# Two transformer blocks on one core: a row scatter spread more densely over the attention heads, and one routing batch's ranks taken three heads earlier

## The chip, the cores and the metric

The kernel runs on one core of one Trainium2 chip. The metric is the device time of one execution in microseconds (us). Five engines work beside each other, each in the order of its own queue: TensorE (PE, with its weight loads shown as PEld), VectorE (DVE), ScalarE (ACT), GpSimd (POOL) and SyncE (SP). They meet only at semaphores.

## The reference, cut to what matters

The input is x with 8 sequences of 256 tokens and 256 features. Block 0 is full attention of 16 heads and a gated low rank layer. Block 1 is causal attention of 16 heads in 4 groups and a mixture of 32 experts, of which each token takes 4, with one more expert that all tokens share:

```python
x = x + attention0(layernorm(x)); x = x + lora_ffn(layernorm(x))
x = x + attention1(layernorm(x))                 # causal, 8 sequences, 16 heads
h = layernorm(x)                                 # 2048 rows of 256
scores = sqrt(softplus(h @ router_w.T))
idx = top_k(scores + expert_bias, 4)
topv = scores[idx] / (scores[idx].sum() + 1e-20)
x = x + sum_k topv[k] * expert[idx[k]](h) + shared_expert(h)
```

The change concerns the way in which rows of h come to their experts.

## The kernel before

**Routing in five batches.** While block 1's attention runs over its 8 sequences (b = 0 to 7, 16 heads each, s = 0 to 15), the sequences that are already through it are routed. `BATCHES` groups them: sequences 0-1, 2-3, 4-5, 6 and 7 are batches 0 to 4 (the change's "second" and "third" batch are batches 1 and 2 by this count). Each batch goes through these steps, at heads given by tables `{(b, s): batch}`: router logits (`LOGITS_AT`, PE), softplus and root (ACT, DVE), the four best experts (`TOP_AT`, DVE), `pick_four` (`PICK_AT`, DVE: L2001 one-hot, L2004 sum, which releases `chosen_ready`), `ranks` on PE and `find_slots` on DVE (both by `RANKS_AT`). `ranks` (L1494 to L1501) counts with matmuls how many rows chose each expert before; `find_slots` (L2020 to L2028) turns that into the row numbers `slot` and releases `slots_ready`.

**The scatter.** For each of a batch's token tiles (128 rows) and each of the four choices, POOL issues one indirect DMA (`scatter`, L890) of 128 rows of 1,040 bytes to DRAM, `rows_by_expert`. That is 16 for each of batches 0 to 2 and 8 for each of batches 3 and 4: 64 in all. `SCATTERS` holds, for batches 0 to 2, (first head by number b*16+s, steps, of, count): scatter n goes behind the exponential of head `first + n * steps // of`. What is left of batch 2 and all of batches 3 and 4 goes behind the loop. SP waits for all 64 to land (`scattered`) before it loads the first block of rows for the experts (L732).

**What else is in POOL's queue.** At head 8 of each sequence stands `scale_rows(b - 1)` (L880, L881), the inverse deviation of the sequence before. ACT's `normalize_row` (L1043) waits for it at heads 9 and 10 of the last sequences, PE's `turn_rows` for that, and so on to the logits. Behind the loop the same step for sequence 7 stands between two of batch 2's scatters.

**The rest around the heads.** Each head is `scores` on PE (L1423, L1426), an exponential on ACT (L1095), and for every four heads `values` on PE (L1447, L1450). Score tiles, router logits, ranks and turned sums share a ring of three PSUM banks, in the order of use that `ring_uses` lists: who takes a bank waits until its use before the last two is read. At head 5 PE turns the sums of the sequence before (`turn_back`, L1461), and DVE divides them and takes row statistics (`divide`, L2035 to L2050, L1957 to L1963). The shared expert's first quarter also lies in the last sequences: its tanh at (7, 1), DVE's `shared_hidden` (L1864, L1868) at (7, 7), PE's `shared_down` (L1540) at (7, 9) and (7, 11).

**Behind the loop** PE does, in this order, `values`, `turn_back(7)`, the shared expert's `shared_up(1)` and `(2)` (L1529), `turn_rows(7)`, logits of batch 4, ranks of batch 3, `shared_down(1)`, `shared_up(3)`, ranks of batch 4, `count` (L1509), `shared_down(2)`. DVE's `find_slots` of batch 4 is followed by the block tables (`count_blocks`, `place_blocks`, L1882 to L1929), which every engine's expert loop needs. In the loop over blocks, rows are read from `rows_by_expert`, multiplied (L1613 to L1635) and scattered again by POOL (L926).

Of the kernel before, what the change touches and what calls it, by code (L numbers as in the profile page):

```python
# [162 lines left out]
SCORES_AT = {(3, 6): 0, (5, 6): 1, (6, 14): 2}  # L163
ROOT_AT = {(3, 8): 0, (5, 8): 1, (6, 15): 2}
TOP_AT = {(3, 10): 0, (5, 10): 1, (7, 0): 2}
PICK_AT = {(3, 13): 0, (5, 13): 1, (7, 2): 2}
RANKS_AT = {(4, 1): 0, (6, 1): 1, (7, 6): 2}
UP_AT, CLIP_AT, TANH_AT, HIDDEN_AT, DOWN_AT, ADD_AT = ((6, 7), (6, 9)), (6, 10), (7, 1), (7, 7), ((7, 9), (7, 11)), (7, 12)
SCATTERS = ((66, 7, 4, 16), (98, 11, 8, 16), (121, 11, 8, 5))


def norms_at(b):
# [3 lines left out]
def rows_at(b):  # L176
    return {SEQS - 2: 11, SEQS - 1: 12}.get(b, 14)


def scatters_at(i):  # L180

    return [(j, n) for j, (first, steps, of, count) in enumerate(SCATTERS) for n in range(count) if first + n * steps // of == i]

# [6 lines left out]
def ring_uses(layer):  # L190
    uses = [("m", 0, 0)]
    for b in range(SEQS):
        for h in range(HEADS):
# [3 lines left out]
            if b + 1 < SEQS and h == TURN_MAX:  # L197
                uses.append(("m", b + 1, 0))
            if layer and (b, h) in RANKS_AT:
                uses.append(("k", RANKS_AT[b, h], 0))  # L200
            if layer and b and h == rows_at(b):
# [23 lines left out]
def two_block_kernel(nc, x_in, wqkv0, wproj, bproj, wffn, debias, wdown, center, slope,  # L225
                     wqkv1, bq1, bk1, bv1, router, ebias, wexp_in, out):
    ctx = ExitStack()
    with ctx:
# [99 lines left out]
        work = cut(exps, 0, TILES * TOPK * EXPERTS, "p (t k e) -> p t k e", t=TILES, k=TOPK)  # L328
        SMALL = ONE_AT + (EXPERTS - 2) * EW
        most = max(size for _, size in BATCHES) * QT * EXPERTS  # L330
        lg, soft, ex, ln = (cut(arena, SMALL + i * most, most, tile_expert, t=most // EXPERTS) for i in range(4))
        sbi = cut(arena, SMALL + 2 * most, most, tile_expert, t=most // EXPERTS)
# [431 lines left out]
        def _(pool):  # L764
# [111 lines left out]
            def scale_rows(b):  # L876

                at = slice(b * QT, (b + 1) * QT)
                pool.wait_ge(rows_var, b + 1)
                then(pool.tensor_tensor(rstd[:, at], var[:, at], mhalf[:, 0:QT], ALU.pow))  # L880
                pool.tensor_tensor(shift[:, at], nmean[:, at], rstd[:, at], ALU.mult).then_inc(rows_scaled, 1)  # L881

            def scatter(j, start, end, after=None):

                pool.wait_ge(slots_ready, j + 1)
                for n in range(start, end):
                    t, k = divmod(BATCHES[j][0] * QT * TOPK + n, TOPK)
                    if after is not None:
                        pool.wait_ge(exp_ready[1], after + 1)
                    pool.indirect_dma_start(xs, bass.IndirectOffsetOnAxis(ap=slot[:, t, k:k + 1], axis=0),  # L890
                                            xn4[:, t, :], None).then_inc(scattered, 16)
# [13 lines left out]
            for b in range(POOL_MASKS, SEQS):  # L905
                for h in range(HEADS):
                    if h == ROWS_VAR:
                        scale_rows(b - 1)
                    for j, n in scatters_at(b * HEADS + h):
                        scatter(j, n, n + 1, b * HEADS + h)  # L910
            scatter(2, SCATTERS[2][3], 7)
            pool.wait_ge(divided[1], SEQS * QT)
            scatter(2, 7, 9)
            scale_rows(7)
            scatter(2, 9, 16)
            scatter(3, 0, 8)
            scatter(4, 0, 8)

# [298 lines left out]
        def _(pe):  # L1217
# [188 lines left out]
            def turn_maxima(n, b):  # L1406
                wait_ring(n, ("m", b, 0))
                pe.wait_ge(neg_ready[n], b + 1)
                dst = st_bank[RING_AT[n]["m", b, 0] % 3]
                for qt in range(QT):  # L1410
                    ins = pe.transpose(dst[0:2 * HEADS, qt * P // 2:(qt + 1) * P // 2].bitcast(BF16),
                                       neg[:, qt, :, :].rearrange("p a h -> p (a h)"), identb[:, :])
                ins.then_inc(negT_ready[n], 1)
# [73 lines left out]
            def ranks(j):  # L1487

                first, size = BATCHES[j]
                t0, n = first * QT, size * QT  # L1490
                wait_ring(1, ("k", j, 0))
                pe.wait_ge(chosen_ready, j + 1)
                dst = st_bank[RING_AT[1]["k", j, 0] % 3]
                pe.matmul(dst[:, 0:n * EXPERTS], before[:, :], chosen[:, t0:t0 + n, :].rearrange("p t e -> p (t e)"),  # L1494
                          start=True, stop=False, skip_group_check=True)
                for t in range(t0):
                    pe.matmul(dst[:, 0:n * EXPERTS], onesb[:, :],
                              chosen[:, t, :].unsqueeze(1).broadcast_to([P, n, EXPERTS]),
                              start=False, stop=False, skip_group_check=True)
                for t in range(1, n):  # L1500
                    ins = pe.matmul(dst[:, t * EXPERTS:n * EXPERTS], onesb[:, :],  # L1501
                                    chosen[:, t0:t0 + n - t, :].rearrange("p t e -> p (t e)"),
                                    start=False, stop=(t == n - 1), skip_group_check=True)
                ins.then_inc(ranks_ready, 1)
# [40 lines left out]
            def attention(n):  # L1545
# [7 lines left out]
                for b in range(SEQS):  # L1553
# [6 lines left out]
                    for s in range(HEADS):  # L1560
# [8 lines left out]
                        if s == TURN_MAX and b + 1 < SEQS:  # L1569
                            turn_maxima(n, b + 1)  # L1570
                        if n and (b, s) in RANKS_AT:
                            ranks(RANKS_AT[b, s])
                        if n and b and s == rows_at(b):
# [115 lines left out]
        def _(dve):  # L1689
# [289 lines left out]
            def top_four(j):  # L1979
                first, size = BATCHES[j]  # L1980
                t0, n = first * QT, size * QT
                dve.wait_ge(root_ready, j + 1)
                step(1, dve.tensor_tensor(sbi[:, 0:n, :], sco[:, t0:t0 + n, :],
                                          ebb[:, :].unsqueeze(1).broadcast_to([P, n, EXPERTS]), ALU.add))
                for t in range(n):
                    ins = dve.max(m8[:, t0 + t, :], sbi[:, t, :])
                step(1, ins)
                for t in range(n):
                    ins = dve.max_index(i8[:, t0 + t, :], m8[:, t0 + t, :], sbi[:, t, :])
                step(1, ins)  # L1990
                step(1, dve.tensor_copy(pk8[:, 0:n, 0:TOPK], i8[:, t0:t0 + n, 0:TOPK]))
                for t in range(n):
                    ins = dve.max(m8[:, t0 + t, :], pk8[:, t, :])
                step(1, ins)
# [58 lines left out]
            def attention(n):  # L2053
                for b, k in first_pairs(n):
                    pair(n, b, k)
                for b in range(SEQS):
                    for s in range(HEADS):
# [12 lines left out]
                        if n and (b, s) in TOP_AT:  # L2070
                            top_four(TOP_AT[b, s])
                        if n and (b, s) in PICK_AT:
                            pick_four(PICK_AT[b, s])
                        if n and (b, s) in RANKS_AT:
                            find_slots(RANKS_AT[b, s])
                        if n and (b, s) == ADD_AT:
# [201 lines left out]
```

## Time and profile before

| what | value |
|---|---|
| median of 3 runs | 653.28 us (646.13, 653.28, 654.76) |
| the profiled execution's own time | 649.37 us |
| its span, first to last instruction | 647.6 us |
| mean granted TensorE clock | 0.951 |
| POOL busy, instructions | 243.1 us (38%), 341 |
| PE busy | 557.5 us (86%) |

Block 1's attention with its routing ends at about 428 us of the span, the first expert block begins at 471 us, and the rest is the expert loop and the final sums. All times of rows below count from the span's start. A timeline row gives start, length, what the instruction is, how many of it were merged, and in brackets how long the engine had been idle and what released it. PE's starts are recorded and its ends modelled, so a semaphore that a matmul sets can be seen by others later than the row suggests.

### The profile page before, as it was taken

To read this page: it belongs to the slowest core of one execution; us is meant where nothing else is said; L and a number is where in the kernel's file an instruction comes from. 1 tells how busy PE (TensorE), PEld (TensorE's weight loads), DVE (VectorE), ACT (ScalarE), POOL (GpSimd) and SP (SyncE) were. 2 spreads that over 40 slices of the span, in tenths; PEclk is the share of its full clock that TensorE was granted. 3 is DMA by queue.
4 is the path that set the end of the run, shared out by engine and by line. 5 is a ranking of instruction groups with operands and counts; after the bars stand their busy time and mean duration, and the time that the engine had idled before them with its cause. 6 is when DMAs were issued, how large, how long until landed. Compare 5 with 4: busy or idle time off the path is not lost.

```text
span 647.6 us, 14149 instructions
## 1 busy us (share of the span) xinstructions
PE 557.5 (86%) x4202; PEld 397.7 (61%) x4203; DVE 431.6 (67%) x1296; ACT 352.7 (54%) x902; POOL 243.1 (38%) x341
## 2 busy tenths in 40 slices
PE   4999898799879789898988987884689999889986
PEld 2565465466458764576756755552567787777864
DVE  4558787688236886676787773452757777767855
ACT  2452476577736578356665546442146665556662
POOL 2353010000603213275545534476525555445530
PEclk9999699899999889999999987798789999989999
DMA  7499879400000006777214151163335454434499
GB/s 249 162 302 284 232 197 271 128 4 2 3 1 1 2 0 179 226 208 229 117 63 171 69 212 68 57 222 148 115 108 149 147 151 144 143 118 147 147 362 343
DMA packets 49536, 95.21 MB, mean 147 GB/s; under 512 B 8580, under 2 KB 40524, under 8 KB 46924
## 3 DMA queue, kind: packets, MB, share of 16 engines
q1 hardware_dynamic: 41804, 75.34, 37.7%
q0 software_dynamic: 7680, 19.21, 7.9%
q8 instruction: 29, 0.48, 0.3%
q14 instruction: 23, 0.19, 0.1%
HBM read 58.54 MB, written 35.59 MB: 145 GB/s over the span
## 4 chain that ended last, share of the span: by engine, by line
PE 45%; DVE 20%; issue 11%; POOL 8%; DMA 7%; ACT 6%; another core or an unknown queue 1%; DVEq 0%; ACTq 0%; POOLq 0%; SPq 0%
PE banks L1423 6%; PE banks L1379 5%; PE banks L1240 4%; POOL rows_by_expert L890 4%; PE banks L1444 4%; DVE mx L1943 3%; PE banks L1315 3%; PE banks L1624 3%; DVE mx L1940 3%; POOL results_by_rank L926 3%; DMA arena<-negT 3%; DVE attn_w L2137 2%; PE banks L1246 2%; DMA arena<-results_by_rank 2%; PE banks L1635 2%
## 5 line engine op out<-in xcount | busy, mean ns | idle before, releaser
L1095 ACT ACTIVATE arena<-banks 128x512 f32<-128x512 f32 (+1 forms) x256 | 130.1, 549 | 88.7 <-PE banks L1423 50.4
L926 POOL DMA_INDIRECT results_by_rank<-attn_w,goes x80 | 78.1, 976 | 82.8 <-issue 49.7
L1423 PE MATMUL banks<-arena 98*128 98x256 bf16 (+1 forms) x512 | 90.5, 271 | 18.1 <-DMA arena<-negT 5.5
L1940 DVE TENSOR_REDUCE mx<-banks 128x4 f32<-128x1024 f32 x64 | 76.1, 1221 | 21.7 <-PE banks L1379 21.6
L1379 PE MATMUL banks<-arena 96*128 96x256 bf16 (+1 forms) x512 | 83.0, 267 | 5.4 <-DVE mx L1940 2.5
L890 POOL DMA_INDIRECT rows_by_expert<-arena,bpb x64 | 63.5, 992 | 59.1 <-ACT arena L1095 26.4
L1624 PE MATMUL banks<-arena,attn_w 128*128 x320 | 84.7, 388 | 0.3 <-issue 0.3
L1423 PEld LDWEIGHTS banks<-arena 98*128 98x128 bf16 x512 | 44.4, 102 | 52.0 <-ACT arena L1095 16.7
L1943 DVE TENSOR_REDUCE mx<-banks 128x4 f32<-128x1024 f32 (+1 forms) x48 | 57.5, 1221 | 20.3 <-PE banks L1383 19.4
L1379 PEld LDWEIGHTS banks<-arena 96*128 96x128 bf16 x512 | 50.6, 100 | 21.6 <-issue 5.6
L1624 PEld LDWEIGHTS banks<-arena,attn_w 128*128 128x128 f32 x320 | 55.9, 195 | 5.3 <-issue 0.9
L1635 PE MATMUL banks<-arena,attn_w 128*128 x160 | 50.5, 397 | 7.2 <-ACT attn_w L1179 3.8
L2137 DVE TENSOR_SCALAR attn_w<-banks 128x256 f32<-128x256 f32 x80 | 34.0, 425 | 29.6 <-issue 14.1
L1167 ACT ACTIVATE attn_w<-attn_w 128x128 f32<-128x128 f32 x80 | 24.8, 310 | 51.6 <-DVE attn_w L2137 41.7
L811 POOL DMA_DIRECT2D arena<-negT x24 | 12.2, 511 | 105.9 <-ACT negT L1027 105.8
L1635 PEld LDWEIGHTS banks<-arena,attn_w 128*128 128x128 f32 x160 | 28.5, 191 | 19.4 <-issue 16.3
L1383 PE MATMUL banks<-mask_s,identb 128*128 128x128 bf16 x256 | 40.1, 220 | 0.0
L1444 PE MATMUL banks<-arena 128*17 128x256 f32 x512 | 35.6, 397 | 1.1 <-ACT pvs L1036 1.1
L1613 PE MATMUL banks<-ident,pvs 128*128 128x128 f32 x160 | 31.6, 280 | 4.1 <-DMA pvs<-rows_by_expert 4.0
L898 POOL TENSOR_SCALAR_AFFINE_SELECT arena<-arena 128x256 f32<-128x256 f32 x64 | 26.2, 420 | 22.8 <-ACT arena L1095 22.7
L803 POOL TENSOR_TENSOR arena<-arena 128x512 bf16<-128x512 f32 x16 | 18.3, 1160 | 41.7 <-ACT arena L938 41.7
L1173 ACT ACTIVATE attn_w<-banks 128x256 f32<-128x256 f32 x80 | 31.0, 387 | 3.1 <-DMA results_by_rank<-attn_w,goes 2.8
(246 smaller groups left out, 1107.8 us busy)
## 6 DMA issues: line engine op xcount, KB each, us to landing
arena<-parts_dram SPq DMA_DIRECT2D x72, 256.0 KB, 4.0
pvs<-rows_by_expert SPq DMA_DIRECT2D x80, 130.0 KB
parts_dram<-arena SPq DMA_DIRECT2D x24, 384.0 KB, 3.0
arena<-results_by_rank SPq DMA_DIRECT2D x6, 1024.0 KB, 10.4
arena<-in SPq DMA_DIRECT2D x2, 2304.0 KB
rows_by_expert<-zero SPq DMA_DIRECT2D x1, 4160.0 KB, 23.4
arena<-in SPq DMA_DIRECT2D x2, 1920.0 KB
arena<-in SPq DMA_DIRECT2D x3, 768.0 KB
```

Source lines behind the costliest of these rows:

```text
L890: pool.indirect_dma_start(xs, bass.IndirectOffsetOnAxis(ap=slot[:, t, k:k + 1], axis=0), xn4[:, t, :], None).then_inc(scattered, 16)
L926: pool.indirect_dma_start(ys, bass.IndirectOffsetOnAxis(ap=goes[:, j:j + 1], axis=0), yb[j], None).then_inc(y_stored[j], 16)
L1095: act.activation(p_ring[n][:, i % P_RING, :], st_bank[RING_AT[n]["s", b, s] % 3][:, 0:P_WIDTH[n]], ACT.Exp, scale=HD ** -0.5).then_inc(exp ...
L1379: ins = pe.matmul(dst[:, a * nk:(a + 1) * nk], q_rows(n, slice(0, STACK), h0 + a, b, qt * P, P), k_rows(n, slice(0, STACK), h0 + a, b, 0, ...
L1383: ins = pe.matmul(dst[:, a * nk + nk - P:(a + 1) * nk], identb[:, :], mask_s[:, :], start=False, stop=True)
L1423: ins = pe.matmul(dst[:, at:at + SEQ - q0], keys, q_rows(n, slice(0, ROWS), s, b, q0, SEQ - q0), start=True, stop=(n == 0 or b < POOL_MASKS))
L1444: ins = pe.matmul(pv_bank[rows, col:col + SEQ], vals, p[:, kt * SEQ:(kt + 1) * SEQ], start=(kt == 0), stop=(kt == QT - 1))
L1624: ins = pe.matmul(bank[2 + p][:, 0:2 * INNER], xbT[:, p, k, :], experts[:, bass.ds(e * EW + k * 2 * INNER, 2 * INNER)], start=(k == 0), st ...
L1635: pe.matmul(bank[6 + p][:, 0:D], hidT[:, p, :], experts[:, bass.ds(e * EW + 2 * KD * INNER, D)], start=True, stop=True).then_inc(y_ready, 1)
L1940: ins = dve.tensor_reduce(out, src.rearrange("p (q h k) -> p q h k", q=QT, k=nk), AX.X, ALU.max)
L1943: ins = dve.tensor_reduce(out, src.rearrange("p (h k) -> p h k", k=nk), AX.X, ALU.max)
L2137: dve.tensor_scalar(gu[:, p, :, :].rearrange("p g i -> p (g i)"), bank[2 + p][:, 0:2 * INNER], CLAMP, -CLAMP, ALU.min, ALU.max).then_inc(g ...
```

## The change

Batch 1's scatters come one for 9/8 heads in place of 11/8, still from head 98. Batch 2's come one for each head from head 117 in place of 11/8 from head 121; so 11 of its 16 stand in the loop in place of 5, and the numbers of the pieces behind the loop follow (2, then 2, `scale_rows(7)`, 1; before 2, then 2, `scale_rows(7)`, 7). Batch 2's `pick_four` moves from (7, 2) to (7, 1), and its `ranks` and `find_slots` from (7, 6) to (7, 3). The ring of PSUM banks follows the tables.

```diff
@@ -163,10 +163,10 @@
 SCORES_AT = {(3, 6): 0, (5, 6): 1, (6, 14): 2}
 ROOT_AT = {(3, 8): 0, (5, 8): 1, (6, 15): 2}
 TOP_AT = {(3, 10): 0, (5, 10): 1, (7, 0): 2}
-PICK_AT = {(3, 13): 0, (5, 13): 1, (7, 2): 2}
-RANKS_AT = {(4, 1): 0, (6, 1): 1, (7, 6): 2}
+PICK_AT = {(3, 13): 0, (5, 13): 1, (7, 1): 2}
+RANKS_AT = {(4, 1): 0, (6, 1): 1, (7, 3): 2}
 UP_AT, CLIP_AT, TANH_AT, HIDDEN_AT, DOWN_AT, ADD_AT = ((6, 7), (6, 9)), (6, 10), (7, 1), (7, 7), ((7, 9), (7, 11)), (7, 12)
-SCATTERS = ((66, 7, 4, 16), (98, 11, 8, 16), (121, 11, 8, 5))
+SCATTERS = ((66, 7, 4, 16), (98, 9, 8, 16), (117, 1, 1, 11))
 
 
 def norms_at(b):
@@ -908,11 +908,11 @@
                         scale_rows(b - 1)
                     for j, n in scatters_at(b * HEADS + h):
                         scatter(j, n, n + 1, b * HEADS + h)
-            scatter(2, SCATTERS[2][3], 7)
+            scatter(2, SCATTERS[2][3], 13)
             pool.wait_ge(divided[1], SEQS * QT)
-            scatter(2, 7, 9)
+            scatter(2, 13, 15)
             scale_rows(7)
-            scatter(2, 9, 16)
+            scatter(2, 15, 16)
             scatter(3, 0, 8)
             scatter(4, 0, 8)
```

POOL's queue from batch 1's scatters on (L890 are scatters, L880 and L881 are the two instructions of a `scale_rows`):

```order
-L890 DMA rows_by_expert<-arena,bpb 65536x260 x8
-L880 TENSOR_TENSOR rstd<-var,mhalf 128x2
-L881 TENSOR_TENSOR shift<-nmean,rstd 128x2
-L890 DMA rows_by_expert<-arena,bpb 65536x260 x11
-L880 TENSOR_TENSOR rstd<-var,mhalf 128x2
-L881 TENSOR_TENSOR shift<-nmean,rstd 128x2
 L890 DMA rows_by_expert<-arena,bpb 65536x260 x9
 L880 TENSOR_TENSOR rstd<-var,mhalf 128x2
 L881 TENSOR_TENSOR shift<-nmean,rstd 128x2
-L890 DMA rows_by_expert<-arena,bpb 65536x260 x23
+L890 DMA rows_by_expert<-arena,bpb 65536x260 x13
```

The piece goes on with `scale_rows` and runs of 12 and 17. So the runs of scatters ahead of `scale_rows(5)`, `(6)`, `(7)` and behind it were 8, 11, 9 and 23 long and are now 9, 13, 12 and 17: six scatters less stand behind `scale_rows(7)`.

DVE's queue in the last sequence, from batch 2's `pick_four` (L2001 to L2008) on; L2020 to L2028 is its `find_slots`, L2035 to L2044 is `divide`:

```order
 L2004 TENSOR_REDUCE products<-arena 128x128
 L2008 SCALAR_TENSOR_TENSOR arena<-ffn_w,tok 128x4x4
+L2020 SCALAR_TENSOR_TENSOR arena<-iota,banks 128x128
+L2025 TENSOR_TENSOR arena<-arena 128x512
+L2027 TENSOR_REDUCE pk<-arena 128x16
+L2028 CAST bpb<-pk 128x16
 L2035 RECIPROCAL rec<-banks 128x16
 L2044 TENSOR_TENSOR arena<-banks,rec 128x256
```

`find_slots` now stands ahead of the divisions and row statistics of sequence 6, where it stood behind them. `pick_four` keeps its place in the queue: nothing stood between (7, 1) and (7, 2).

PE's queue in the last sequence, around the place where the ranks of batch 2 (L1494 to L1501) now stand; each four rows of L1423 and L1426 are one head's scores, L1461 is `turn_back`:

```order
 L1501 MATMUL banks<-products,onesb 128x64
 L1501 MATMUL banks<-products,onesb 128x32
+L1423 MATMUL banks<-arena 128x256
+L1426 MATMUL banks<-mask_t,identb 128x128
+L1423 MATMUL banks<-arena 128x128
+L1426 MATMUL banks<-mask_t,identb 128x128
+L1423 MATMUL banks<-arena 128x256
+L1426 MATMUL banks<-mask_t,identb 128x128
+L1423 MATMUL banks<-arena 128x128
+L1426 MATMUL banks<-mask_t,identb 128x128
+L1461 MATMUL banks<-ident,pvs 128x128 x8
+L1423 MATMUL banks<-arena 128x256
```

The added rows, the scores of heads 4 and 5, `turn_back(6)` and the scores of head 6, stood ahead of the ranks and now stand behind them.

## Rows read from the trace of the kernel before

**Rows 1.** Cores view: span and mean granted TensorE clock.

```profile
core 0: 647.6 us, clock 0.951
```

**Rows 2.** Chain of work ending last, 395 to 430 us: start, length, what.

```profile
408.39 0.22 PE banks L1494
...
410.36 0.30 DVE arena L2020
...
412.94 0.70 DVE attn_w L1868
413.68 2.07 PE banks L1540 x4
```

**Rows 3.** The same chain, 436 to 472 us.

```profile
451.05 3.68 issue
...
464.31 4.06 DMA rows_by_expert<-arena,bpb
...
469.13 2.16 DMA pvs<-rows_by_expert
```

**Rows 4.** Timeline, POOL: start, length, engine, line, operation, tiles [idle before <-releaser].

```profile
409.37 0.72 POOL L880 TENSOR_TENSOR rstd<-var,mhalf 128x2 f32<-128x2 f32 x1
...
412.74 1.08 POOL L890 DMA_INDIRECT rows_by_expert<-arena,bpb  x1 [2.37 <-DVE bpb L2028]
...
425.06 0.99 POOL L890 DMA_INDIRECT rows_by_expert<-arena,bpb  x1 [0.30 <-issue]
428.05 1.29 POOL L890 DMA_INDIRECT rows_by_expert<-arena,bpb  x1 [2.00 <-DVE arena L2044]
...
430.62 0.73 POOL L880 TENSOR_TENSOR rstd<-var,mhalf 128x2 f32<-128x2 f32 x1
...
441.20 0.96 POOL L890 DMA_INDIRECT rows_by_expert<-arena,bpb  x1 [0.30 <-issue]
...
450.08 0.96 POOL L890 DMA_INDIRECT rows_by_expert<-arena,bpb  x1 [0.30 <-issue]
454.95 1.15 POOL L890 DMA_INDIRECT rows_by_expert<-arena,bpb  x1 [3.90 <-DVE bpb L2028]
```

**Rows 5.** Source view of the scatter line.

```profile
L890 POOL DMA_INDIRECT rows_by_expert<-arena,bpb x64: 957/963/1428, 343.4 to 464.3; - x64
```

**Rows 6.** Timeline, ACT.

```profile
403.28 0.87 ACT L1095 ACTIVATE arena<-banks 128x384 f32<-128x384 f32 x2
```

**Rows 7.** Timeline, DVE.

```profile
402.26 1.02 DVE L2004 TENSOR_REDUCE products<-arena 128x128 bf16<-128x512 f32 x1
...
405.63 0.26 DVE L2035 RECIPROCAL rec<-banks 128x16 f32<-128x16 f32 x1 [2.27 <-PE banks L1461]
...
409.11 0.18 DVE L1963 TENSOR_SCALAR nmean<-mv 128x2 f32<-128x2 f32 x1
...
437.95 0.38 DVE L2028 CAST bpb<-pk 128x8 uint32<-128x8 f32 x1
...
442.13 0.68 DVE L1860 TENSOR_SCALAR attn_w<-banks 128x512 f32<-128x512 f32 x1
453.33 0.22 DVE L2020 SCALAR_TENSOR_TENSOR arena<-iota,banks 128x64 f32<-128x64 f32 x1 [10.53 <-remote]
...
466.50 0.14 DVE L1922 TENSOR_SCALAR trips_i<-trips_i 1x1 int32<-1x1 int32 x1
```

**Rows 8.** Timeline, PE.

```profile
403.82 0.39 PE L1423 MATMUL banks<-arena 98*128 98x256 bf16 x1 [2.63 <-ACT arena L1095]
...
409.26 0.37 PE L1501 MATMUL banks<-products,onesb 128*128 128x96 bf16 x3
...
413.68 2.07 PE L1540 MATMUL banks<-arena,attn_w 128*128 128x256 f32 x4 [2.52 <-DVE attn_w L1868]
...
445.11 0.18 PE L1501 MATMUL banks<-products,onesb 128*128 128x32 bf16 x1
...
446.20 0.21 PE L1509 MATMUL banks<-products,onesb 128*128 128x32 bf16 x2 [0.55 <-issue]
```

## The prediction, made before the changed kernel ran

> **What bounds the kernel now.** I read the page first: one core, 647.6 us of span, PE busy for 86% of it at a mean granted clock of 0.951 [rows 1]. PE's share is an average over stages, so I went on to the chain of waits in the two stretches that the change touches. In the last sequence of block 1's attention [rows 2] the chain goes from batch 2's ranks on PE (408.39) to `find_slots` on DVE (410.36), on to the shared expert's hidden product (412.94, ended 413.64), and back to PE's `shared_down` at 413.68: there PE stands behind a DVE queue. Behind the attention [rows 3] the chain is POOL's scatters, one by one, then 3.68 us of POOL idle at 451.05, the last eight scatters, 4.06 us from the last one's start to its landing, and 2.16 us of the first block's load. Everything of the expert loop stands behind that. Then the timelines of POOL, DVE, ACT and PE one at a time, to see who has slack.
>
> What is to be seen in POOL's [rows 4]: the last scatter ahead of the final division runs at 425.06, two follow the division from 428.05 on, `scale_rows(7)` runs at 430.62, and from there 15 scatters run without a gap: seven of batch 2, then batch 3's eight from 441.20 to 451.04. That is a full queue: batch 3's row numbers were made at 438.33 [rows 7] (the cast at 437.95) and waited 2.9 us for POOL. Batch 4's eight begin at 454.95, for they had to wait for their row numbers.
>
> **The change, part by part.**
>
> *Batch 2's ranks and slots at head 3.* The pick at (7, 1) in place of (7, 2) moves nothing: DVE has nothing between the two. Its sum ended at 403.28 [rows 7], so the ranks at head 3 can begin on PE at about 403.4. PE was idle there anyway: it waited 2.63 us, until 403.82, for the exponential that ACT could only begin at 403.28 [rows 6, 8]. The ranks take 1.24 us (408.39 to 409.63 [rows 2, 8], at the lower clock) and so end at 404.65. What is late next are the scores of heads 4 and 5 and `turn_back(6)`, which stand behind them: scores of head 5 from about 405.1 in place of 403.82, so up to 1.3 us late. In return PE is rid of the same 1.24 us at 408.39, and stands level again by head 7. `find_slots` starts 0.73 us behind the ranks' last row (409.63 to 410.36), so at 405.4. With the two hidden products of 0.70 each it took 410.36 to 413.64, so alone 1.9: it ends at 407.3. The divisions and statistics of sequence 6, which started at 405.63 and were through at 409.29 (3.66 us [rows 7]), now start at 407.3 and end at 411.0. The hidden products follow at once and end at 412.4 in place of 413.64: **1.2 us sooner**, and PE waits for exactly these. `scale_rows(6)` moves from 409.37 to about 411.9, since it also has a scatter ahead of it; ACT normalizes at heads 9 and 10, and PE turns those rows only at head 12, behind 2.07 us of `shared_down` [rows 2] and three heads, so I cost this at nothing. If that cover is gone it costs PE 1.3 to 2.6 us.
>
> *Denser scatters in the loop.* Scatters do not block PE, DVE or ACT, and a scatter ahead of `scale_rows` costs it at most one pace. Batch 1 is through about 4 us sooner (three heads' worth). Batch 2's row numbers come at 407.3, where its first scatter ran at 412.74 before [rows 4]. From there to the end of the attention, which now comes at about 426.8, are 19.4 us. The 13 scatters and `scale_rows(6)` that POOL has to do in them need 13 times the full queue's pace of 1.27 us (below) and 1 us, 17.5 in all, so POOL keeps up. No more instructions are issued: 64 scatters before and after, 957/963/1428 ns at least, in the middle and at most [rows 5].
> The Trainium skill (SBUF — State Buffer, section "SBUF: two separate sides") speaks against such a move: it says that POOL and DVE share a pair of SBUF ports, locked by one for a whole instruction, so that descriptors for POOL's own DMAs may wait for a DVE instruction in a two-port mode. By it, six scatters moved from a stretch in which DVE idles to one in which it works could each be as long as the longest row, 1.43 in place of 0.96, or 2.8 us of POOL. The row's middle of 963 ns, with most of the 64 beside DVE's work, speaks for nothing, and where they now stand POOL waits for exponentials anyway.
>
> *Six scatters less behind `scale_rows(7)`.* The pace in a full queue is (450.08 - 441.20) / 7 = 1.27 us, so six are 7.6 us of POOL. But one of the terms comes short: batch 3's row numbers. They hang on `scale_rows(7)`, which moves with the 1.2 us of the attention from 430.62 to 429.4, and so come at 437.1. POOL does the one scatter left and then idles until 437.15. Batch 3's scatters thus start at 437.15 in place of 441.20 and end at 447.0 in place of 451.04: **4.05 us sooner**, of which 1.2 are those above.
>
> *Batch 4's start* decides what of this reaches the end. Before, DVE's `find_slots(4)` began at 453.33 after 10.53 us of idle, though PE's rows of the ranks end at 445.29 and those of the count at 446.41 [rows 7, 8]. The releaser is not told. So PE's semaphore came 8 us behind its row, for a reason that the trace does not show. Bounds from both sides: a hold of fixed length moves by 1.2 only; no hold at all puts the row numbers at about 446, ahead of POOL, and batch 4's start moves from 454.95 to 447.3, by 7.65. Between them: the hold ended 2.3 us behind the last scatter of batch 3 (451.04), and if it goes with the scatters all moves by 4.05. If ordinary executions have no such hold, before had POOL at 451.35 and the changed kernel has it at 447.3, which is 4.05 again. I take **4.05**, which two of the four readings give.
>
> Behind it nothing else ends later: the block tables on DVE (453.33 to 466.64, 13.3 us [rows 7]) start from the same semaphore as batch 4's row numbers and are through 1.7 us before the last scatter lands (464.31 + 4.06 = 468.37 [rows 3]). That keeps its distance.
>
> **The sum.** 649.37 - 4.05 = 645.3 against the profiled execution's own time (span 647.6 and 1.8 around it). The median of the runs, 653.28, lies 3.9 above it, and their lowest, 646.13, 3.2 below. The four times of the kernel have a mean of 650.9, and I put the forecast there: 650.9 - 4.05 = 646.9, said as 647.
>
> **The rivals.**
>
> *The hold stays as long as it is* (25%). PE's count and ranks are the same, and so is what stands ahead of them. Then the tail gains only the 1.2 us: 649.7. For it speaks that batch 4's first scatter was released by DVE and not by POOL's own queue; against it that no hold of this size stands behind batch 3's ranks, with nearly as many matmuls.
>
> *The hold goes* (15%). It would belong to this one execution, or to PE's work beside a full POOL queue. Then 7.65 us: 643.2.
>
> *Slower: PE waits at head 3* (18%). The ranks at head 3 stand ahead of heads 4 and 5, which ACT would otherwise have begun at 403.82 and before. If the 1.3 us on `turn_back(6)`, and a further 1.3 us because `find_slots` stands ahead of the divisions and a scatter ahead of `scale_rows(6)`, are not caught up, then the attention ends 2.6 us later, and with a hold of fixed length so does everything: 653.5. It decides from the point where PE's head 9 scores (their bank waits for sequence 6's divisions two uses before) start later than 411.0, so that `shared_down` no longer waits for DVE. Against it: PE waited there 2.52 us for DVE before [rows 8].
>
> *The change does nothing to time* is the case of the first rival without its 1.2 us and is counted there.
>
> **How the numbers follow.** Forecast 42%, the others as above. The range should hold 8 in 10: its low end is 643.2 less 1.5 for the spread of a median, which I take as half of the 3.2 by which the lowest run lies under the profiled one; the high end is 653.5 and 1. So 641.7 to 654.5. 2% of the time is 13 us, about what a measurement of this kernel can tell from no change; even the best case lies within it. Only where it falls together with a set of low runs is the change faster by that much (5%), and slower by 2% needs 13 us that no case has (2%).
>
> **What would show it.** In the changed kernel's profile: PE's ranks rows (L1494) in the idle gap at about 403.4, `shared_down` waiting about 1.2 us for DVE instead of 2.5, `scale_rows(7)` at about 429.4, POOL idle for some 6 us between the one scatter behind it and batch 3's first at about 437, and batch 4's first close behind batch 3's last. Wrong would be: the first block later than 469.5 (then the hold or the wait at head 3), or `scale_rows(7)` at 431 or later (then the in-loop part failed and the gain from the tail is at most what POOL's queue gives).

## The result: slower by 0.9% where the forecast was faster by 0.6%

| | before | after |
|---|---|---|
| median (20 runs each, side by side) | 650.31 us | 654.44 us |
| span of the profiled execution | 647.6 us | 652.8 us |
| granted clock | 0.951 | 0.953 |

The ratio is 1.0092, with a 95% interval of 1.0067 to 1.0116. It compares fast runs alone, the slower state being left out, and is not the quotient of the two medians, which is 1.0064. The forecast of 647.0 was the mean of the kernel's four times then known, 650.9, less 4.05 us. The time lies at the upper edge of the range, but its direction is that of the rival with 18%, and the mechanism is neither the forecast's nor that rival's.

The cores of the kernel after, which answer to [rows 1]:

```profile
core 0: 652.8 us, clock 0.953
```

POOL's timeline of the kernel after, as [rows 4] (start, duration, line, idle time before it with what ended it):

```profile
414.93 0.73 POOL L880 TENSOR_TENSOR rstd<-var,mhalf 128x2 f32<-128x2 f32 x1
...
416.46 1.04 POOL L890 DMA_INDIRECT rows_by_expert<-arena,bpb  x1 [0.52 <-issue]
417.80 0.96 POOL L890 DMA_INDIRECT rows_by_expert<-arena,bpb  x1 [0.30 <-issue]
...
424.14 0.96 POOL L890 DMA_INDIRECT rows_by_expert<-arena,bpb  x1 [0.31 <-issue]
427.93 0.96 POOL L890 DMA_INDIRECT rows_by_expert<-arena,bpb  x1 [2.83 <-ACT arena L1095]
...
435.12 0.73 POOL L880 TENSOR_TENSOR rstd<-var,mhalf 128x2 f32<-128x2 f32 x1
...
436.28 1.04 POOL L890 DMA_INDIRECT rows_by_expert<-arena,bpb  x1 [0.16 <-issue]
444.12 0.96 POOL L890 DMA_INDIRECT rows_by_expert<-arena,bpb  x1 [6.80 <-DVE bpb L2028]
...
454.39 1.15 POOL L890 DMA_INDIRECT rows_by_expert<-arena,bpb  x1 [0.43 <-DVE bpb L2028]
...
463.46 0.96 POOL L890 DMA_INDIRECT rows_by_expert<-arena,bpb  x1 [0.30 <-issue]
```

Three things are to be seen. Seven scatters now follow each other without a gap while the attention still runs (416.46 to 425.10). `scale_rows(7)` comes at 435.12 and not at 429.4. And what was foretold for the tail is there in form: one scatter, 6.80 us of idle time, batch 3, and batch 4 right behind it. The last scatter even starts sooner than before (463.46 against 464.31). POOL's queue is thus not what made it late.

Rows of ACT, of DVE and of PE in the kernel after, from their timelines:

```profile
426.66 0.49 ACT L1095 ACTIVATE arena<-banks 128x384 f32<-128x384 f32 x1 [6.11 <-remote]
467.00 1.09 ACT L1060 ACTIVATE arena<-banks 128x512 f32<-128x512 f32 x2 [9.47 <-remote]
```
```profile
407.50 0.29 DVE L2020 SCALAR_TENSOR_TENSOR arena<-iota,banks 128x128 f32<-128x128 f32 x1 [3.36 <-remote]
426.60 0.22 DVE L1969 COPY arena<-banks 128x64 f32<-128x64 f32 x1 [8.25 <-remote]
...
464.07 0.19 DVE L1882 COPY wd<-banks 128x32 f32<-128x32 f32 x1 [7.21 <-remote]
...
473.10 0.15 DVE L1925 SCALAR_TENSOR_TENSOR stored_i<-wd,iota 1x12 int32<-1x12 f32 x1
```
```profile
404.20 0.27 PE L1494 MATMUL banks<-products,before 128*128 128x128 bf16 x1 [2.82 <-DVE products L2004]
...
414.13 1.13 PE L1540 MATMUL banks<-arena,attn_w 128*128 128x256 f32 x4 [0.60 <-DVE attn_w L1868]
...
469.31 2.02 PE L1517 MATMUL banks<-ident,vec 128*128 128x96 f32 x8 [7.12 <-DVE vec L1908]
...
478.41 0.63 PE L1613 MATMUL banks<-ident,pvs 128*128 128x128 f32 x4 [1.62 <-ACT arena L1060]
```

"Remote" marks a wait whose releaser is not told. By the program these are waits for a semaphore of PE's, and it came long after its matmul's row: the count's rows (L1509) end at 451.2, and DVE goes on at 464.07. As the ends of PE's rows are modelled, they do not tell whether the matmuls ended late or only their semaphores came late; "late semaphore" stands for both below. Before, there was one such wait of size, the 10.53 us of [rows 7]. Now ACT's exponential waits 6.11 us and DVE's copy 8.25 us beside the seven scatters, and in the tail DVE's count 7.21 us and ACT's turned sums 9.47 us beside the last sixteen. The attention's last statistics end at 434.41 instead of 429.91 (+4.5 us), the block tables at 473.4 (one row behind the last shown) instead of 466.9, the same instruction (+6.5), and the first block starts at 478.41 instead of 471.33 (+7.1). The way from the late count to the first block is in PE's rows: PE waits 7.12 us for a value of the tables (L1517, 469.31), `shared_down(3)` stands behind that in its queue, ACT takes its result (`L1060`), and PE's first block waits for ACT, no longer for the scattered rows. The expert blocks give 1.9 us back, and the span is 5.2 us longer.

### The profile page after: what moved, and what is told of

Its sections match the earlier page's. It is cut to its first block, busy times and chain, and to the rows that moved or that the text cites. A ratio compares the mean times of both kernels' runs of the same rounds, so it can differ in the third digit from the quotient of the medians.

```text
span 652.8 us, 14155 instructions
## 1 busy us (share of the span) xinstructions
PE 556.3 (85%) x4202; PEld 395.7 (61%) x4203; DVE 431.2 (66%) x1296; ACT 352.5 (54%) x902; POOL 243.2 (37%) x341
## 4 chain that ended last, share of the span: by engine, by line
PE 42%; DVE 23%; issue 10%; ACT 7%; DMA 7%; POOL 5%; another core or an unknown queue 4%; DVEq 0%; ACTq 0%; POOLq 0%; SPq 0%
PE banks L1423 5%; PE banks L1379 4%; PE banks L1240 4%; PE banks L1624 4%; DVE mx L1943 3%; PE banks L1444 3%; DMA arena<-negT 3%; DVE mx L1940 3%; PE banks L1315 3%; POOL results_by_rank L926 3%; PE banks L1246 2%; PE banks L1635 2%; DMA arena<-results_by_rank 2%; DVE attn_w L2137 2%
## 5 line engine op out<-in xcount | busy, mean ns | idle before, releaser
L1423 PE MATMUL banks<-arena 98*128 98x256 bf16 (+1 forms) x512 | 90.2, 270 | 18.9 <-DMA arena<-negT 7.3
L890 POOL DMA_INDIRECT rows_by_expert<-arena,bpb x64 | 63.6, 994 | 57.6 <-ACT arena L1095 27.3
L1624 PE MATMUL banks<-arena,attn_w 128*128 x320 | 82.6, 381 | 0.7 <-ACT attn_w L1162 0.4
L1423 PEld LDWEIGHTS banks<-arena 98*128 98x128 bf16 x512 | 43.8, 101 | 53.8 <-ACT arena L1095 13.9
L1624 PEld LDWEIGHTS banks<-arena,attn_w 128*128 128x128 f32 x320 | 54.5, 190 | 5.3 <-issue 1.2
L1635 PE MATMUL banks<-arena,attn_w 128*128 x160 | 50.0, 394 | 7.4 <-ACT attn_w L1179 3.8
L1635 PEld LDWEIGHTS banks<-arena,attn_w 128*128 128x128 f32 x160 | 28.2, 189 | 19.6 <-issue 16.5
```

What stands on the lines that cost most here:

```text
L1423: ins = pe.matmul(dst[:, at:at + SEQ - q0], keys, q_rows(n, slice(0, ROWS), s, b, q0, SEQ - q0), start=True, stop=(n == 0 or b < POOL_MASKS))
L1624: ins = pe.matmul(bank[2 + p][:, 0:2 * INNER], xbT[:, p, k, :], experts[:, bass.ds(e * EW + k * 2 * INNER, 2 * INNER)], start=(k == 0), st ...
L1635: pe.matmul(bank[6 + p][:, 0:D], hidT[:, p, :], experts[:, bass.ds(e * EW + 2 * KD * INNER, D)], start=True, stop=True).then_inc(y_ready, 1)
```

## The experiments

The kernels ran in sets, each set on one chip, with runs of the kernel before among them; a ratio is to those, with its 95% interval. A "650 us set" is one in which before takes about 650 us (its median was 649.9 and 652.3 in the two below, 650.3 in the result), a "634 us set" one in which it takes 632.8 to 634.8. That there are two kinds was not expected, and turned out to be the main finding. The experiments stand in the order in which they ran.

### First set (650 us): which part of the change costs

The part that moves the ranks alone (`e1`):

```diff
-PICK_AT = {(3, 13): 0, (5, 13): 1, (7, 2): 2}
-RANKS_AT = {(4, 1): 0, (6, 1): 1, (7, 6): 2}
+PICK_AT = {(3, 13): 0, (5, 13): 1, (7, 1): 2}
+RANKS_AT = {(4, 1): 0, (6, 1): 1, (7, 3): 2}
```

> The picks, ranks and slots of batch 2 as in the changed kernel, all scatters as before. Theory R (an unbroken run of POOL's scatters holds back the arrival of PE's semaphores): nothing runs back to back in the last eight heads, so no 6 us gap behind the logits; time as before or up to 1.2 us less (ratio 0.998 to 1.000). Theory P (the new place of ranks in PE's queue makes the stall): the gap of about 6 us on ACT behind head 14 of the last sequence is there, ratio about 1.008. Theory N (the stalls fall by chance and the two kernels differ by their tails): gap or not by chance, ratio within 0.5% of before.

Measured: 649.21 us, 0.9972 [0.9934, 1.0010]. The ranks' new place does not cost the 0.9%. In its trace the wait of before ahead of batch 4's slots is still there (10.6 us), and none over 1.1 us lies in the last two sequences. From the first statistics of block 1 to the last ones the attention takes 125.8 us, against 128.3 in before and 132.2 in the kernel after (one trace each).

The change with batch 1's scatters left as before (`e2`), and batch 1's alone (`e3`):

```diff
-SCATTERS = ((66, 7, 4, 16), (98, 9, 8, 16), (117, 1, 1, 11))    # after
+SCATTERS = ((66, 7, 4, 16), (98, 11, 8, 16), (117, 1, 1, 11))   # e2
-SCATTERS = ((66, 7, 4, 16), (98, 11, 8, 16), (121, 11, 8, 5))   # before
+SCATTERS = ((66, 7, 4, 16), (98, 9, 8, 16), (121, 11, 8, 5))    # e3
```

> The changed kernel with batch 1's scatters at 11/8 heads again, batch 2's still one for each head from head 117. Theory R: POOL's run in the last eight heads stays (it is even longer, since batch 1's last ones lie there too), so the gap of 5 to 6 us stays and the ratio is 1.008 or more. Theory P: the same as the changed kernel, 1.009. Theory N: within 0.5% of before. If batch 1's density were the cause, the ratio would be 1.000 or less.

> The kernel before with batch 1's scatters one for 9/8 heads and nothing else changed. Theory R: POOL is a little denser in sequence 6, runs of three to six scatters; a gap of 1 us at most, ratio 1.000 to 1.003. Theory P: ratio 1.000. If it carries the loss: 1.006 or more.

Measured: e2 1.0049 [1.0013, 1.0084], e3 1.0036 [1.0001, 1.0070]. Each seems to carry a part. But the controls below read 0.9956 and 0.9976 for the kernel before against itself, so neither is told from 1 for certain. What e2's trace shows is surer. It has the same run of seven scatters, ACT's exponentials wait 13.0 us there in three waits, and the tables are late as in the kernel after (472.3); e3, without the run, has one wait of 2.4 us of ACT's and one of 10.7 of DVE's in the tail, like before.

Spaced scatters (`e4`): in the kernel after, POOL clears an unused tile and waits for it behind each scatter.

```diff
                                             xn4[:, t, :], None).then_inc(scattered, 16)
+                    then(pool.memset(zero[:, :], 0.0))
```

> The changed kernel with a memset of 128x512 on POOL behind every scatter, waited for, so that a full queue has one scatter in about 2.0 us in place of 1.27. More work for POOL: 64 x 0.7 us. Theory R: the holds behind the logits (6 us) and in the tail (2 to 12 us) go or shrink to under 2 us, while POOL's queue itself grows: its 17 scatters behind the loop take 12 us more, so the time is still 2 to 8 us above the changed kernel; the test is whether PE's semaphores arrive on time. Theory P or N: holds of the same size at the same places, and the time 10 us or more above the changed kernel.

Measured: 660.87 us, 1.0141 [1.0088, 1.0193]. Scatters in a full queue now come 1.79 us apart and not 1.27. No wait for "remote" is left in the last sequences, and the attention of sequence 7 takes 16.3 us from the statistics before to its own, in place of 21.7 in the kernel after. The spacing costs more at the end: batch 4's last scatter is through at 474.7.

### Second set (650 us): how much spacing

Before with e4's spacing (`e5`), after with a memset of 128x4 (`e6`), after with e4's spacing inside the attention only (`e7`), after with 128x256 (`e8`).

> The kernel before with the same waited memset of 128x512 behind every scatter (a full queue's pace was 1.79 us in the paced version of the changed kernel, not 2.0). Theory R: no hold over 1 us is left on PE's semaphores; the 10.5 us gap of DVE ahead of batch 4's slots goes, the attention's last sequence takes 16 to 17 us between the row statistics of sequences 6 and 7 in place of 20.6, but 23 scatters behind the loop take 12 us more, so ratio 1.005 to 1.015. Theory N (chance): the 10.5 us gap stays and the ratio is 1.02 or more.

> The changed kernel with a waited memset of only 128x4 behind every scatter: pace about 1.35 us, queue broken all the same. If the hold comes from the pace (transfers or descriptors too dense), the holds stay as in the changed kernel (6, 4 and 7 us) and the ratio is 1.009 to 1.013. If it comes from POOL's queue running ahead without a wait between scatters, they go, and since the tail is hardly longer the time is 3 to 8 us under the kernel before: 0.988 to 0.996.

> The changed kernel with the waited memset of 128x512 behind the scatters of the loop alone; behind the loop they run at 1.27 us as ever. Theory R: no hold behind the logits of the last sequence, the holds in the tail (4 and 7 us at batch 4's slots and at the counts) come back. POOL, late with its in-loop scatters, is late with the last sequence's scale_rows by 3 to 8 us. Ratio 1.000 to 1.010. Theory P: the hold behind the logits stays.

> The changed kernel with a waited memset of 128x256: pace about 1.55 us. Between the two others: if the hold grows with density, holds of 0.5 to 3 us are left; if 1.55 us is slow enough, none, and the time is 2 to 6 us under the fully paced version, ratio 1.004 to 1.010.

| kernel | pace in a full queue | ratio | waits for "remote", 335 to 490 us | sequence 7, statistics to statistics |
|---|---|---|---|---|
| e5 | 1.79 us | 1.0073 [1.0030, 1.0117] | none | 16.4 us |
| e6 | 1.36 | 1.0017 [0.9974, 1.0060] | ACT 23.2 us, DVE 18.7 | 21.3 |
| e7 | 1.79, tail 1.27 | 1.0041 [1.0006, 1.0076] | one in the tail, 5.7 | 16.0 |
| e8 | 1.57 | 0.9994 [0.9953, 1.0035] | none | 14.7 |

The kernel after has 17.0 us of ACT's and 24.0 of DVE's in the same stretch. So in these sets the waits come with scatters 1.27 to 1.36 us apart and are gone at 1.57. The profiles of e5 and e6 are of runs at a lower clock (0.942 and 0.938), which is why little more than their waits is read. e7 shows that the waits of the attention and of the tail are separate: each goes where its own scatters are spaced. What the waits cost in time is less clear. e8 is level with before, but the kernel after did not run in this set, and e6, which has all the waits, reads 1.0017, with an interval that overlaps e8's. That the waits are what makes the kernel after slower is thus read from the path in its trace, and not shown by these ratios.

### Third set (634 us): meant to beat both

`c1`: spaced by 128x256, and `scale_rows(7)` ahead of all that is left of batch 2. `c2`: the same with batch 4 unspaced. `c3`: c1 with 128x128 (1.46 us in a full queue). c1 against the kernel after, three places of it:

```diff
-SCATTERS = ((66, 7, 4, 16), (98, 9, 8, 16), (117, 1, 1, 11))
+SCATTERS = ((66, 7, 4, 16), (98, 9, 8, 16), (117, 1, 1, 10))
 ...
+                    then(pool.memset(zero[:, 0:256], 0.0))
 ...
-            scatter(2, SCATTERS[2][3], 13)
-            pool.wait_ge(divided[1], SEQS * QT)
-            scatter(2, 13, 15)
             scale_rows(7)
-            scatter(2, 15, 16)
+            scatter(2, SCATTERS[2][3], 16)
```

> A version built on the theory: the changed kernel's tables with 10 of batch 2's scatters in the loop in place of 11, the waited memset of 128x256 behind every scatter (pace 1.57 us as measured), and scale_rows(7) first behind the loop, ahead of the six scatters left. Theory R: no hold of PE's semaphores; scale_rows(7) at the moment its statistics are ready, 6 us sooner than in the version with the same pace, so batch 3's slots at about 435 and the last scatter issued at about 462 after a start like before's: first expert block 2 to 4 us sooner than before, ratio 0.993 to 0.998. Theory N: holds at the old places and ratio 1.00 or more.

> The same without the memset behind the last eight scatters (batch 4), which then take 10.3 us in place of 12.6. Theory R: PE's counts have arrived before these begin, and only the shared expert's sums come late, which nothing waits for in the first 4 us; first block 2 us sooner than in the version above, ratio 0.990 to 0.995. If the hold catches the counts or the spread values, the tables are late and the ratio is 1.000 or more.

> The first version with a memset of 128x128, a pace of about 1.43 us. Theory R with a hold that grows with density (1.27 us: 5 to 13 us, 1.33 us: 4 to 7 us, 1.57 us: none): some hold of 1 to 4 us is back, while POOL is 4 us shorter over its last 31 scatters; ratio 0.990 to 1.000.

Measured: 1.0107 [1.0076, 1.0139], 1.0066 [1.0029, 1.0104] and 1.0027 [0.9996, 1.0058]. All three missed. Yet no trace of the three has a late semaphore, and c1's first block starts at 465.6, 5.7 us sooner than before's 471.33. The answer had to be in the kernel before, which took 632.8 us in this set.

### Fourth and fifth set (634 us): the kernels before and after again

Both kernels unchanged, twice each; c3 once more; e8 once more.

> The kernel before, unchanged, profiled in the same call as the kernel after and the paced kernel with the scaling first. In the last call all three paced kernels lost 0.3 to 1.1% against a kernel before of 632.8 us, although none of their traces has a held-back semaphore and their first expert block starts 4 to 8 us sooner than in the trace of before that I have (471.33), which is of a run of 649.4 us. If the held-back semaphores are what the kernel before always pays (theory), this trace again has DVE's wait of about 10 us for the write mask's semaphore and its first expert block near 471, and its gain on a chip where it runs in 633 us lies in the expert blocks. The rival: the waits come and go with the chip, and where before runs in 633 us its trace has none in the last batches and its first block comes near 460.

> The kernel after, unchanged, on the same chip as the kernel before. Theory: 1.005 to 1.012 of before, with ACT's, DVE's or PE's waits of 5 to 10 us behind the seven scatters in a row that follow head 120 and again in the counts of the last batch; tables about 6 us after those of before. Rival (the waits belong to one chip): no wait over 3 us in the last sequence, and the loss, if any, comes from POOL's queue.

> The kernel after with the smallest spacing (a waited memset of 128x128 behind each scatter), eleven of the third batch's scatters ... ten of them in the loop, and the scaling of the last sequence first behind it. If the spacing is a cure and the last call's 1.0027 was the chip's, it comes out at 0.990 to 0.997 where before shows its wait of 10 us (first block at 464 against 471); if before shows none in this call, at 1.000 to 1.006.

> The kernel before, unchanged, as a control of what the ratios can tell: its ratio to itself should be 1 within 0.4% either way. The chip matters: with a median near 650 us, ACT's and PE's waits for nothing shown (10 us of ACT's at L1167 in the expert blocks) and DVE's or ACT's waits of 5 us and more in the last two sequences return; near 634 us none of them.

> The kernel after, unchanged. Theory (dense scatters hold the other engines back on some chips alone): 1.005 to 1.012 of before on a chip where before takes 650 us, with waits of 5 to 10 us in the trace; 0.996 to 1.002 on one where before takes 634 us, with none. Rival: the loss has nothing to do with the chip, and the two results so far (1.0092 and 0.9985) are the spread of one number near 1.003.

> The kernel after with a waited memset of 128x256 behind each scatter (1.57 us a scatter where they follow each other). Theory: where before takes 650 us, 0.995 to 1.001 of it and 0.5 to 1% under after in the same call; where before takes 634 us it only costs, 16 scatters of the last two batches by 0.30 us each on the path: 1.005 to 1.010. Rival: the same ratio on either.

| kernel | ratio |
|---|---|
| before against itself | 0.9956 [0.9918, 0.9994], 0.9976 [0.9948, 1.0003] |
| after | 0.9985 [0.9958, 1.0011], 0.9959 [0.9929, 0.9990] |
| c3 | 1.0050 [1.0025, 1.0075] |
| e8 | 1.0210 [1.0170, 1.0251] |

The rival of n1 held: the waits are not the kernel's alone. In the traces of these sets none of PE's semaphores is late, of either kernel. Here the change costs nothing and brings nothing that can be told: both of its ratios lie where before's own do. From the first statistics of block 1 to the last, the attention takes 121.7 and 120.5 us in before (n1, n4) and 119.8 and 120.1 in after (n2, n5), where it took 128.3 and 132.2 in the first traces. The controls also show what a ratio can tell: one of the two misses 1 by 0.0044, more than its interval allows. e8, which was level with before in the 650 us set, loses 2.1% here.

The same group of ACT's in the expert blocks (480 to 640 us), first of the kernel before in its first trace, then of n1 and n5. Columns: line, operation, count, busy time, mean ns, idle time before and what ended it. The count is of the rows that the trace kept.

```profile
L1167 ACT ACTIVATE attn_w<-attn_w 128x128 f32<-128x128 f32 x76 | 23.6, 310 | 47.5 <-DVE attn_w L2137 37.7 <-issue 9.7
```
```profile
L1167 ACT ACTIVATE attn_w<-attn_w 128x128 f32<-128x128 f32 x71 | 22.0, 309 | 44.1 <-DVE attn_w L2137 44.1
```
```profile
L1167 ACT ACTIVATE attn_w<-attn_w 128x128 f32<-128x128 f32 x69 | 21.4, 310 | 42.7 <-DVE attn_w L2137 42.7
```

The 9.7 us in which ACT waited for nothing that the profile shows are there in the 650 us sets alone (7.0 to 10.5 us in their ten traces, none in the other ten). The two kinds of set are the same program in two conditions: the kernel before takes 15 to 19 us more in the one, the kernel after 21 to 23. Little of this lies in the expert blocks. n1's span is 14.4 us shorter than that of the first trace; 7.0 of them are there when the attention ends (422.96 for 429.92), 12.1 when the first block starts (459.23 for 471.33), and 2.3 come behind it. The clock has a small part in it at most, for PE's busy time is 554.0 us for 557.5.

POOL's timeline of n4, the kernel before in a 634 us set, and of n5, the kernel after in the same set:

```profile
404.66 1.04 POOL L890 DMA_INDIRECT rows_by_expert<-arena,bpb  x1 [1.55 <-DVE bpb L2028]
...
418.41 1.28 POOL L890 DMA_INDIRECT rows_by_expert<-arena,bpb  x1 [0.71 <-DVE arena L2044]
420.00 0.96 POOL L890 DMA_INDIRECT rows_by_expert<-arena,bpb  x1 [0.30 <-issue]
420.98 0.72 POOL L880 TENSOR_TENSOR rstd<-var,mhalf 128x2 f32<-128x2 f32 x1
...
431.47 0.96 POOL L890 DMA_INDIRECT rows_by_expert<-arena,bpb  x1 [0.31 <-issue]
...
451.18 0.96 POOL L890 DMA_INDIRECT rows_by_expert<-arena,bpb  x1 [0.30 <-issue]
```
```profile
402.71 0.96 POOL L890 DMA_INDIRECT rows_by_expert<-arena,bpb  x1 [1.57 <-DVE bpb L2028]
...
409.63 1.04 POOL L890 DMA_INDIRECT rows_by_expert<-arena,bpb  x1 [0.52 <-issue]
410.97 0.96 POOL L890 DMA_INDIRECT rows_by_expert<-arena,bpb  x1 [0.30 <-issue]
...
423.63 0.96 POOL L890 DMA_INDIRECT rows_by_expert<-arena,bpb  x1 [0.30 <-issue]
424.61 0.73 POOL L880 TENSOR_TENSOR rstd<-var,mhalf 128x2 f32<-128x2 f32 x1
...
432.09 0.96 POOL L890 DMA_INDIRECT rows_by_expert<-arena,bpb  x1 [5.28 <-DVE bpb L2028]
...
451.71 1.04 POOL L890 DMA_INDIRECT rows_by_expert<-arena,bpb  x1 [0.30 <-issue]
```

In n5 twelve scatters follow each other from 409.63 on, 1.27 us apart, a longer run than the seven of the kernel after in its 650 us set, and nobody is held. So dense scatters alone do not make the waits. The rows show a second thing: `scale_rows(7)` starts at 424.61, though the statistics that it reads ended at 420.76; in n4 they ended at 420.26 and it ran at 420.98. Batch 3's row numbers come late by that, and POOL idles 5.28 us. The six scatters fewer behind it are eaten up: batch 3 starts at 432.09 against 431.47, in traces whose first statistics already lie 0.8 us apart.

n6's loss works out from the same rows. Spaced, POOL's queue is further behind inside the attention (`scale_rows(7)` at 434.03 for 424.61) and batch 3 starts at 442.93 for 432.09. That is 10.8 us, less the 1.6 by which n6's first statistics are late. The last 16 scatters add 0.30 us each (4.8). Together they are 14.0, and its span is 15.3 longer than n5's, 13.7 without the 1.6. My expectation had only the second part.

### Sixth set (634 us): the late scaling taken away

c1 without any spacing: ten of batch 2's scatters in the attention, then `scale_rows(7)`, then the other six.

> The kernel after with ten instead of eleven of the third batch's scatters in the loop and scale_rows(7) right behind them, ahead of the other six, without any spacing. Theory (where nothing is held back, the change gains nothing because scale_rows(7) stands behind three more queued scatters, at 424.61 against statistics that end at 420.8, and batch 3's row numbers so come 3.7 us late while POOL idles 5.28 us): on a chip where before takes 634 us, scale_rows(7) within 1 us of the statistics, POOL's idle time before batch 3 under 2 us, batch 4's last scatter 3 to 4 us sooner, ratio 0.991 to 0.997. On a chip where before takes 650 us the dense run of scatters is still there: 1.000 to 1.010. Rival (the end is set by DVE's block tables and PE's shared expert, not by POOL's queue): POOL's last scatter comes sooner but the first block does not, 0.996 to 1.002 on the fast kind of chip.

Its POOL timeline:

```profile
419.52 0.96 POOL L890 DMA_INDIRECT rows_by_expert<-arena,bpb  x1 [0.30 <-issue]
423.63 0.72 POOL L880 TENSOR_TENSOR rstd<-var,mhalf 128x2 f32<-128x2 f32 x1 [3.15 <-DVE nmean L1960]
...
432.85 0.96 POOL L890 DMA_INDIRECT rows_by_expert<-arena,bpb  x1 [0.30 <-issue]
...
451.96 0.96 POOL L890 DMA_INDIRECT rows_by_expert<-arena,bpb  x1 [0.30 <-issue]
```

Measured: 630.99 us, 0.9970 [0.9938, 1.0003]. The scaling is on time (statistics' end 423.55), and POOL has no idle time ahead of batch 3. Counted from the first statistics of block 1, which come at 303.29 here, at 299.81 in n4 and at 300.62 in n5, the last scatter is through at 149.6 us (n4 152.3, n5 152.1), the first block starts at 154.0 (156.7, 157.2), and the last instruction ends at 326.2 (328.3, 328.6). That is 2 to 3 us in one trace each, in line with the ratio, but the controls read as low. The late scaling is thus shown as the cause of POOL's idle time. That c4 beats the kernel before is not shown, and no version here does so beyond doubt.

## Why the prediction was wrong, point by point

- **The ranks at head 3** came as foretold: PE ran them at 404.20 in an idle gap, `shared_down` waited 0.60 us for DVE in place of 2.52 (414.13, [rows 8]). The 1.2 us that it was to bring did not come, for `find_slots` began at 407.50 and not at 405.4, since PE's semaphore came late, and the hidden products ended at 414.07 and not at 412.4. The rival that put the loss there falls with e1 (0.9972).
- **The step that failed is the one costed at nothing**: "Scatters do not block PE, DVE or ACT, [...] so POOL keeps up". In the 650 us condition the first half is false. Waits of 6.11 us (ACT) and 8.25 us (DVE) stand beside the seven scatters; the sequence from statistics to statistics takes 21.7 us, against 16.0 with the spacing of e7, and the attention ends 4.5 us later.
- **The second half is false in either condition.** I counted 13 scatters and 1 us, 17.5 of 19.4 us. But 15 scatters stand ahead of `scale_rows(7)`, the two behind the `divided` wait included: 15 times 1.27 and 1 are 20.05 us. In n5 there were 18.05 from batch 2's first scatter (402.71) to the statistics (420.76), and POOL also stood 1.28 and 0.83 us for exponentials early on. So the scaling came 3.85 us late. That `scale_rows(7)` "moves with the 1.2 us of the attention" was therefore wrong, and with it the 4.05 us. Where nothing is held back no gain can be told (ratios 0.9985 and 0.9959, the controls 0.9956 and 0.9976). c4, which takes this wait away, shows the cause of POOL's idle time.
- **"The hold"** of 8 us behind batch 4's ranks was the clue and was read too narrowly. I treated it as one event of fixed place, to be moved or not. It was the sign of a condition in which such waits come beside dense runs of scatters, and with six scatters moved into the attention one came there too, which goes when these are spaced (e7). The second rival ("the hold goes") describes the 634 us sets, where both kernels lack it: n4 has batch 4 right behind batch 3, as that rival had it. Its gain of 7.65 us did not come there either, since before has no hold to lose.
- **The block tables: "That keeps its distance"** is false, and so is its ground, that they "start from the same semaphore as batch 4's row numbers". In the kernel the row numbers wait for `ranks_ready` and the tables for `counts_ready`, which `count` sets behind the ranks. In the run shown the first came at 452.70 and the second at 464.07, after a wait of 7.21 us. The tables ended at 473.4, 5 us behind the landing that I had reckoned with before (468.37), and the first block waited for ACT (`L1060`), not for rows.
- **The Trainium skill's rule** on DVE's and POOL's ports, weighed in the prediction at up to 2.8 us, changed nothing: the middle scatter is 963 ns as before, and the longest 1451 ns against 1428. The same page (the Trainium skill, SBUF — State Buffer, section "Who interferes with whom") also says that PE and ACT never wait on anyone. ACT's 6.11 us and 9.47 us were, by the program, waits for PE's semaphore, so they do not contradict that rule on ports; no run here shows which resource delayed PE.

## What to carry to other kernels

Work costed at nothing because it lies on another engine needs two proofs: that the engine's own queue has room for all that stands ahead of its next urgent instruction, waits included, and that the rows around it show nobody waiting for a cause that the trace does not name. A wait whose releaser is not told, 8 us behind its matmul, is a cost of the stage and its condition; ask what runs beside it before moving more of that there. And run the kernel before again, profiled, in each set: a version without the waits that was level in one condition (e8, 0.9994) was a loss of 2.1% in the other.

## What the runs showed of the hardware that was not expected

- The same kernel takes 650 us in some sets and 633 us in others, at nearly the same granted clock (0.951 in the first trace, 0.958 in n1). The condition lasted through a set: the runs of before lie between 644.9 and 659.6 us in the two 650 us sets and between 628.3 and 640.0 in the four others. It is not shown to belong to a chip: e5 to e8 (before 652.28) and c4 (before 632.89) ran on chips of the same number. What sets it stays open.
- In the 650 us condition, PE's semaphores arrive up to 13 us behind their matmuls' rows (single waits of up to 10.7 us) beside indirect scatters 1.27 to 1.36 us apart, and not at 1.57 or 1.79 us. In the 634 us condition, twelve and more in a row at 1.27 us hold nobody. Which resource it is was not tried: to thin out the scatters' rows would have changed which rows the experts read.
- A scatter takes POOL 0.96 us and follows the last one after 0.30 us, in either condition. What differs is what the others can do meanwhile.
